# The G products of a feature-interaction tower as full-f32 half-height matmuls, with x's diagonal written by a mask product

## The reference

```python
for W in (W0, W1):
    Wr = W.reshape(m, Hk, Hn)                       # m = 39; Hk = 39, then 128; Hn = 128
    xk = jnp.einsum('bid,bjd,ijh->bhd', x0, xk, Wr)
    outs.append(xk)
z = jnp.sum(jnp.concatenate(outs, axis=1), axis=-1) # sum over d
h = relu(concat([z, dense_ctx]) @ W_top1 + b_top1)
h = relu(h @ W_top2 + b_top2)
y = h @ W_top3
```

## Time and profile before

| what | us |
|---|---|
| median of 3 runs (range) | 386.85 (385.5 to 388.55) |
| the profiled execution | 384.8 |
| its span | 383.0 |
| PE busy | 238.1 |
| DVE busy | 164.6 |
| ACT busy | 162.5 |
| POOL busy | 121.4 |

### The profile page before, as it was taken

How to read it: one execution, slowest core, us unless ns; L and a number is a source line. 1 busy time by engine, 2 the same in 40 slices (tenths; PEclk the granted TensorE clock), 3 DMA queues, 4 the chain that set the end, 5 groups by cost and what they waited for, 6 DMA issues and landing times. The chain is left out here.

```text
span 383.0 us, 4943 instructions
## 1 busy us (share of the span) xinstructions
PE 238.1 (62%) x1749; PEld 192.2 (50%) x1749; DVE 164.6 (43%) x336; ACT 162.5 (42%) x312; POOL 121.4 (32%) x119
## 2 busy tenths in 40 slices
PE   3662711011000011006988999999999999999997
PEld 2662400000000010004765778977799777888887
DVE  6943700000100000022887976755857656756211
ACT  6943510000000000014888577665868747756201
POOL 5987777777777777400000000000000000000000
PEclk9995765555555555555999999999999999999999
DMA  7600191000000000002020011000000100010000
GB/s 164 189 6 14 25 254 28 6 7 7 6 7 7 6 7 6 5 7 70 12 70 16 16 21 19 5 14 17 15 15 9 19 9 13 16 19 17 2 0 2
DMA packets 29094, 10.94 MB, mean 29 GB/s; under 512 B 21274, under 2 KB 27252, under 8 KB 29070
## 3 DMA queue, kind: packets, MB, share of 16 engines
q1 hardware_dynamic: 25390, 9.68, 11.0%
q0 software_dynamic: 3680, 0.95, 2.8%
HBM read 7.99 MB, written 0.00 MB: 21 GB/s over the span
## 5 line engine op out<-in xcount | busy, mean ns | idle before, releaser
L788 ACT ACTIVATE prod<-pair_bank 128x512 f32<-128x512 f32 (+1 forms) x112 | 66.1, 600 | 174.1 <-remote 119.8
L334 POOL DMA_INDIRECT emb<-tbl,ids_sb x115 | 121.2, 1054 | 37.2 <-issue 34.8
L414 PE MATMUL x_turn_bank<-tab_parts,later_hot 125*128 125x48 bf16 x160 | 12.5, 190 | 96.4 <-issue 95.7
L377 PE MATMUL x_bank<-prod_hi,pair_w_hi 128*128 128x512 f32 (+1 forms) x112 | 64.3, 574 | 6.9 <-issue 3.7
L651 DVE TENSOR_TENSOR prod_lo<-prod,prod_hi 128x512 fp32r<-128x512 f32 x96 | 65.0, 687 | 3.4
L414 PEld LDWEIGHTS x_turn_bank<-tab_parts,later_hot 125*128 125x128 bf16 x160 | 7.9, 100 | 102.1 <-issue 101.1
L359 PE MATMUL pair_bank<-x,sel 117*128 117x512 bf16 (+1 forms) x112 | 45.4, 406 | 9.7 <-issue 7.1
L641 DVE CAST prod_hi<-prod 128x512 fp32r<-128x512 f32 x48 | 20.4, 426 | 72.0 <-ACT prod L788 71.7
L633 DVE TENSOR_SCALAR later_hot<-later_ids,row_id 125x1024 bf16<-125x1024 f16 x20 | 9.7, 495 | 94.3 <-remote 94.2
L380 PE MATMUL x_bank<-prod_hi,pair_w_lo 128*128 128x512 f32 x96 | 38.9, 406 | 5.1 <-issue 5.1
L424 PE MATMUL turn_bank<-g_sb,w_sb 128*128 128x128 f32 x312 | 41.4, 275 | 0.6 <-ACT g_sb L820 0.6
(11 more groups left out here) (126 smaller groups left out, 307.1 us busy)
## 6 DMA issues: line engine op xcount, KB each, us to landing
xblk<-xs SPq DMA_DIRECT2D x128, 20.0 KB
emb<-tbl,ids_sb POOLq DMA_INDIRECT x115
tab<-small SPq DMA_DIRECT2D x2, 560.0 KB
wt<-w_top SPq DMA_DIRECT2D x2, 512.0 KB, 4.0
tab<-small SPq DMA_DIRECT2D x1, 504.0 KB
wa<-pair_w_a SPq DMA_DIRECT2D x1, 448.0 KB, 3.2
wb<-pair_w_b SPq DMA_DIRECT2D x1, 448.0 KB, 4.0
sel<-select SPq DMA_DIRECT2D x1, 204.8 KB
```

What stands on the lines that cost most here:

```text
L334: pool.indirect_dma_start(out=emb[:, at:at + D], out_offset=None, in_=tables[f], in_offset=bass.IndirectOffsetOnAxis(ap=ids_sb[:, c * M + ...
L377: mm = pe.matmul(x1_bank[:, :], pair_w_hi[p, t, :], hi(n), start=(t == 0), stop=(t == FULL))
L414: mm = pe.matmul(x1_turn_bank[:, f * 3 * D:(f + 1) * 3 * D], later_hot[:, r % HOT, f, :], tab_parts0[:, f, r, :, :], start=(r == 0 and f = ...
L788: act.activation(prod[0:ROWS[t], n % RING, :], pair_bank[n % 2][0:ROWS[t], :], ACT.Square).then_inc(sq_done, 1)
```

## The change

- **Layout of x3.** A group of 8 samples becomes two half groups of QB = 4. Turned rows of a group are now (half, d, b): rows 0 to 63 for four samples, rows 64 to 127 for the other four.
- **G.** `contract_d(k, pair)` takes two groups at a time. For each group and each half it issues one full-f32 matmul over 64 rows and 160 columns (4 samples x 40). The lower rows write `g_bank` 0, the upper ones `g_bank` 1. There is no hi/lo split. G_AT = (3, 6): both calls stand inside the same block's steps. A call waits for both copies (ACT's and DVE's) of the call before.
- **x's diagonal.** `spread_x` on DVE multiplies the turned x, repeated over four samples, with the mask `own` (128 x 4) and writes 128 x 4 x 4 x 39 numbers of `xblk` in one instruction. `xblk` is f32 with three buffers; its column of ones is written once from `own`. The 128 DMAs on SP, ACT's rounding of x, DVE's remainder of x and the zeroing of `xs` and `xblk` are gone.
- **x1.** ACT copies it to `x1_t` in f32; DVE's two remainder instructions are gone.
- **Copies of G.** ACT copies bank 0 and DVE bank 1 after each call, 128 x 320 each.

```diff
-G_AT = (3, 4, 6)
+G_AT = (3, 6)
...
+QB = GB // 2
+QC = MO * QB
+HALF = D * QB
+XBUFS = 3
...
-            def spread(k):
-
-                sp.wait_ge(xs_lo_done, k + 1)
-                wait(sp, g_mm, NG * (k - 1))
-                for b in range(GB):
-                    sp.dma_start(xblk[b::GB, k % 2, :, :, b, :].rearrange("p q g i -> p (q g) i").bitcast(F32),
-                                 xs[b::GB, k % 2, :, :, :].rearrange("p q g i -> p (q g) i").bitcast(F32)
-                                 ).then_inc(xblk_done[k % 2], 16)
...
-            def contract_d(k, g):
-                if g == 0:
-                    pe.wait_ge(x1_rounded, k + 1)
-                    pe.wait_ge(xblk_done[k % 2], SPREAD * (k // 2 + 1))
-
-                wait(pe, g_dve if g % 2 else g_act, 2 * k + g // 2)
...
+            def contract_d(k, pair):
+
+                if pair == 0:
+                    pe.wait_ge(x1_done, k + 1)
+                    pe.wait_ge(xblk_done, k + 1)
+
+                wait(pe, g_act, 2 * k + pair)
+                wait(pe, g_dve, 2 * k + pair)
+                for at in range(2):
+                    g = 2 * pair + at
+                    for half in range(2):
+                        rows = slice(half * HALF, (half + 1) * HALF)
+                        mm = pe.matmul(g_bank[half][:, at * QC:(at + 1) * QC], x1_t[rows, g * H:(g + 1) * H],
+                                       xblk[rows, k % XBUFS, g, :, :].rearrange("p b i -> p (b i)"), start=True, stop=True)
+                mm.then_inc(g_mm, 1)
...
+            def spread_x(k):
+
+                dve.wait_ge(xt_done, k + 1)
+                wait(dve, g_mm, 2 * (k - XBUFS + 1))
                 x_turned = misc_bank[:, 0:NG * MO].rearrange("p (g i) -> p g i", g=NG)[:, :, 0:M]
-                dve.tensor_tensor(xs[:, k % 2, 1, :, 0:M], x_turned, xs[:, k % 2, 0, :, 0:M],
-                                  ALU.subtract).then_inc(xs_lo_done, 1)
-
-            def take_x1_lo(k):
-                dve.wait_ge(x1_rounded, k + 1)
-                for half in (slice(0, NG // 2 * H), slice(NG // 2 * H, NG * H)):
-                    dve.tensor_tensor(x1_lo[:, half], x1_turn_bank[:, half], x1_hi[:, half],
-                                      ALU.subtract).then_inc(x1_done, 1)
...
+                dve.tensor_tensor(xblk[:, k % XBUFS, :, :, 0:M], x_turned.unsqueeze(2).to_broadcast([128, NG, QB, M]),
+                                  own[:, :].unsqueeze(1).unsqueeze(3).to_broadcast([128, NG, QB, M]),
+                                  ALU.mult).then_inc(xblk_done, 1)
```

More of the change, by code:

```diff
@@ L103, in build_tower @@
         parts = sb("parts", [128, D, 3, M], BF16)
-        x3 = sb("x3", [P3, 2, NB * NG, D, GB], BF16)
-        xs = sb("xs", [128, 2, 2, NG, MO], F32R)
-        xblk = sb("xblk", [128, 2, 2, NG, GB, MO], F32R)
+        x3 = sb("x3", [P3, 2, NB * NG * 2, D, QB], BF16)
+        own = sb("own", [128, QB])
+        xblk = sb("xblk", [128, XBUFS, NG, QB, MO])
         with ExitStack() as early:
@@ L268, in lo, with g_cols, g_bank_cols @@
             return prod_lo[:, n % RING2, :] if n % NT < FULL else prod_hi[32:64, n % RING2, :]
-        def g_cols(k, g):
-            b0 = (k % NB) * BB + g * GB
-            return g_sb[:, k // NB % 2, :, b0:b0 + GB]
+        def g_cols(k, pair, half):
+            b0 = (k % NB) * BB + pair * 2 * GB
+            return g_sb[:, k // NB % 2, :, b0:b0 + 2 * GB].rearrange("p i (g h b) -> p i g h b", g=2, b=QB)[:, :, :, half, :]
+        def g_bank_cols(half):
+            return g_bank[half][:, 0:2 * QC].rearrange("p (g b i) -> p i g b", g=2, b=QB)
         block = ctx.enter_context(nc.Block())
@@ L290, in _ @@
             sp.dma_start(row_id[:, :, :], row_ids).then_inc(row_id_in, 16)
+            sp.dma_start(own[:, :], own_row).then_inc(own_in, 16)
             for n, (f0, w, rows) in enumerate(SETS):
@@ L303, in _ @@
             sp.dma_start(idf[:, :], ident_f).then_inc(idf_in, 16)
[L304 to L308, removed]
+            for k in range(3):
+                sp.wait_ge(xblk_done, k + 1)
                 if k == 0:
@@ L362, in turn_x @@
             def turn_x(k):
-                wait(pe, xs_lo_done, k)
+                wait(pe, xblk_done, k)
                 pe.wait_ge(x3_b, k // NB + 1)
@@ L384, in turn_x1 @@
                 pe.wait_ge(x1_kept, k + 1)
-                wait(pe, x1_done, 2 * k)
+                wait(pe, x1_done, k)
                 c, j = divmod(k, NB)
@@ L479, in step @@
                     select_pair(n)
-                if u == 0 and k >= 2:
-                    contract_d(k - 2, 3)
                 if m >= 0:
@@ L567, in _ @@
             step(TILES + 3)
-            contract_d(K - 2, 3)
             mlp2(NCH - 2)
@@ L571, in _ @@
             mlp3(NCH - 2)
-            pe.wait_ge(xs_lo_done, K)
+            pe.wait_ge(xblk_done, K)
             for m in range(M1):
                 h1_part(NCH - 1, m, 0, True)
-            for g in range(NG):
-                contract_d(K - 1, g)
+            for pair in range(2):
+                contract_d(K - 1, pair)
             layer2(NCH - 1, 0, M)
@@ L930, in _ @@
             keep_x1h(K - 1)
-            keep_g(K - 2, 2)
+            keep_g(K - 2, 1)
             relu2(NCH - 2)
```

103 lines of the change are left out of this document (36 added, 67 removed).

## The result

The changed kernel takes 403.68 us (median of 4 runs, 400.32 to 407.23) against 386.24 us for the kernel before (4 runs, 385.5 to 388.55): a ratio of 1.040, 95% interval 1.035 to 1.046. It is slower, by far more than the 1% that was forecast. That the time lies inside the forecast's range, 374 to 404 us, is luck: the range reached so far for halves that run one after the other, and that is not what happened. The ratios in this text compare only runs within 1.5% of the fastest of their kernel, the medians take all runs. The profiled execution took 400.32 us with a span of 398.5 us, against 383.0 us before.

The account below looks back on a forecast made before the run. PE was taken to bound the dense part; the slow stretch had no named cause. Terms of +9.5, -1.0, -2.2 and -2.0 summed to +4.3 us on the median of 386.85, about 391 us, range 374 to 404 us.

Parts of the forecast that it names:

- The slow stretch: Early stretch of nearly idle PE: 16 fewer SP DMAs of x give back a few turns, -2 us, ends 0 and -6.
- The start: Chunk 0's gathers: without the memset of `xblk` that holds POOL, all comes earlier, -2.2 us, ends 0 and -2.3.
- A call's eight records: PE in `contract_d`: eight f32 records cost 0.79 us a call, ends 0.70 and 1.12, without changes of height.
- The change of height: PE around each `contract_d` call: going to 64 rows and back costs 0.19 us each, 0.39 us a call.
- +9.3 us stood for thirty: Thirty calls of `contract_d` in the dense part, each 1.18 us against 0.87 us before: +9.3 us.
- In the rest of chunk 0 ... -1.0 us together: From 174.3 to 209.0 us: three blocks gain 0.3 us each on ACT, PE's idle absorbs some new work; ends 0 and -3.
- The tail: The last block's two calls of G and their copies, with nothing overlapping: 3.16 us against 2.96, +0.2 us.
- Behind 209 us this is hidden: Dense part: savings of 0.36 us a block on DVE and 0.296 on ACT lie under PE and are worth nothing.
- Serial halves: Rival in `contract_d`: the two halves don't work side by side, 1.51 us a call, 401 us in all; chance 0.25.
- Cheap change of height: Rival in `contract_d`: 64 rows cost no change of height and the halves overlap, 0.70 us a call, 376 us; chance 0.18.
- The stretch hangs on SP's DMAs of x: Rival: the slow stretch goes with those DMAs, up to 120 us of its 127.5, leaving about 270 us; chance 0.08.
- for what I don't see: Remaining chance of 0.07, for example a slower copy of G or x3, or a longer slow stretch.

Follow-up runs that it names:

- f2: The kernel before, unchanged, run once more with its own trace on the next chip: 387.7 us.
- e2: The kernel before with the second memset of `xblk` moved ahead of the one-hots, into idle DVE time: 395.35 us, ratio 1.025.
- e1: The changed kernel with the 2.19 us memset put back on DVE behind the one-hots, into a tile nobody reads: 390.6 us.
- e7: The kernel before without the indirect gathers of chunks 1 to 3 (one plain DMA per chunk instead): 253.5 us.
- e3: The changed kernel without the indirect gathers of chunks 1 to 3 (one plain DMA per chunk instead): 265.4 us.
- f1: The changed kernel, unaltered, run once more on the next chip: 402.9 us, ratio 1.048.
- e14: The changed kernel without gathers of chunks 1 to 3, each product of G over all 128 rows: 1.09 us a call, no whole time given.
- e15: The changed kernel without gathers of chunks 1 to 3, all products of G over rows 0 to 63: 1.28 us a call, no whole time given.
- e13: The changed kernel with a POOL memset of 128 x 512 ahead of each gather of chunks 1 to 3, on another chip: 305.1 us, ratio 1.135.
- f3: The changed kernel with at most two gathers in flight and, from chunk 1 on, each tied to the tiles: 300.9 us, ratio 0.772.

## Why the prediction was wrong, point by point

- **The slow stretch ("PE's instructions before and inside it stay what they are", "-2 us, ends 0 and -6"): the step that failed.** The instructions stayed, the stretch's place among them did not. It began at 20.2 us, inside the third lookup, in place of 46.8, and put some 19 us of dense work behind it; with an end 4.6 us earlier that is +14.4 us where -2 stood. (In f2 the start moved by 20 us and block 0 did not, with the third lookup and nearly all touch matmuls through. So it is the work caught, and not the time of the start alone.) The profile of before had what was needed and I used it for another term only: the earlier trace rows show POOL held for 2.3 us just as the third lookup runs, and POOL's gathers as the only thing that goes on through the whole stretch (84.87 us busy in the earlier trace rows). I took the hold for a pure loss and asked only what an earlier gather gains, not what it collides with.
- **The start ("-2.2 us")**: that the memset holds a gather was right: without it the gather at 18.11 us takes 0.95 us. It is the 8th, not the 7th that the prediction named as its sign; the 7th takes 6.30 us there, as the 6th took 7.88 before. The last gather of chunk 0 is 4.3 us earlier, 2.3 us by the hold and the rest mostly because one gather more is issued ahead of 18 us. The worth was of the wrong sign: by block 0's transposes the hold saved 11.5 us in e2 (190.29 against 178.75) and 12.4 in e1 (193.17 against 180.73).
- **A call's eight records ("I take the middle of these two, 0.79 us")**: 0.55 us. Both estimates were too high. The lower one assumed that four records can't pair fully in this order, the other that two weight loads stand no closer than 0.11 us; that spacing is of loads into the same rows.
- **The change of height (2 x 0.19)**: 0.38 us measured, against 0.39. The row of a 16-row matmul priced a 64-row one within 0.01 us.
- **So a call costs 0.93 us and not 1.18**, where +9.3 us stood for thirty. The 0.87 us of before was too low as well. It took both groups at 0.43 us; the group behind `turn_x` costs 0.53, since its first matmul takes 0.24 us and not 0.15 (the chain of waits, before):

```profile
213.71 0.11 PE misc_bank L367 x4
213.82 0.24 PE g_bank L403
214.06 0.14 PE g_bank L404
214.21 0.15 PE g_bank L407
```

  So two groups cost 0.92 us on the mean. Blocks 8 to 15 give +0.5 us for 14 calls, about +0.04 a call or +1 us for thirty.
- **"In the rest of chunk 0 ... -1.0 us together"**: not shown. The blocks' +1.3 is made of -1.4 over blocks 0 to 3 (31.6 us before, 30.2 after), +1.6 at block 4 and +1.0 over blocks 4 to 15 (139.7 and 140.7 us). Of these the first doesn't repeat: it is -0.6 between e7 and e3, and +0.9 between f2 and f1. From block 0 to block 15 these pairs give +2.0 and +2.6 us.
- **The tail ("+0.2 us")**: from the start of the last block's G to the end of the last copy 2.84 us against 2.96, -0.1.
- **"Behind 209 us this is hidden"**: not in one place. In block 4 the one-hots of the next chunk stand behind the mask product and a copy of G in DVE's queue, and PE waits 1.68 us for one where it waited 0.73; the granted clock dips behind it (0.76 from 233 to 240 us). From block 3 to block 4 it is 12.0 us before and 13.6 after; in f2 and f1, without the dip, 12.0 and 12.9.

```profile
233.16 0.37 PE L409 MATMUL x_turn_bank<-tab_parts,later_hot 125*128 125x48 bf16 x8 [1.68 <-DVE later_hot L626]
```

- **The rivals.** "Serial halves" is refuted by e14 and e15. "Cheap change of height" is refuted as to its mechanism, but its price (0.70 us) was a little nearer to 0.93 than mine (1.18). "The stretch hangs on SP's DMAs of x" is refuted by the changed kernel itself, which has none of them and 149.5 us of the stretch; its time of 270 us is near what e3 and e7 gave when the gathers went, and what the kernel before took on one chip. What happened was in the 0.07 "for what I don't see", as "a longer slow stretch". The test I named ("wrong if the slow stretch differs by more than 6 us") is met: 149.5 against 127.5 us. So is the other, that the dense part be 6 to 10 us longer: it is 1.3 us longer by the blocks.

The page "TensorEngine Tiling (Array Packing)" of the Trainium skill states under "Key Properties" that a change of mode drains TensorE and that tiles can run their weight loads and matmuls in parallel. The runs agree with both halves, at 0.19 us a change and 0.55 against 1.09 us a call.

## What stays open

What the gathers and the instruction supplies share isn't named by any row. The trace's packets that carry instructions don't show it either: in the changed kernel one such packet starts between 22 and 175 us (8 KB at 50.3 us, 0.71 us long), so PE does not wait for one slow transfer of them after the other. Why that start of PE's work, the third lookup and the touch matmuls, matters more than what follows was not tested. On the chips where the kernel before takes 387 us the number in flight and the pitch were never moved apart (e13 ran on another). Why one chip of those used ran the kernel before in 269 us wasn't found; no trace of that kernel was taken there, and the changed kernel wasn't run there. Whether the version of f3 can be made better on both kinds of chip was not tried.

## What to carry to other kernels

When a profile shows one engine idle with "issue" as its reason, first ask which stream runs about as long as that idleness, and what work of the idle engine stands ahead of it, and treat their order as something that your change can move: an edit that only relieves that stream's engine can then cost more than all that it saves. A stream of small gathers may be worth slowing down: spreading the same 101 gathers over the tiles made the kernel 20% faster than before (0.795, 0.780 to 0.809) on a chip where the stretch exists, and a similar bound made it 6.6% slower on one where it doesn't, so both must be measured. Half-height f32 products on the two halves of the array are worth twice their rate, less 0.19 us each time the height changes.

## What the hardware showed that was not expected

- While POOL issues indirect gathers at a pitch of 1.25 us, PE's and SP's instructions come late: on PE 94 matmuls in 149.5 us (at first in groups of some five, 1.5 us apart, as at 20.88 and 22.34 us above), and in one run ACT's and DVE's too. Without the gathers of chunks 1 to 3 the long stretch is gone, and at a pitch of 2.6 us PE was not slowed. The slowness outlasts the last gather by 16 to 18 us (157.9 to 174.3 before, 152.1 to 169.7 after), though its data is there after 2.0 us.
- The low granted clock is not part of it: 145 us of it ran at 1.00 in f1.
- A 2.19 us memset on DVE, there for its zeros, was worth 12 us at block 0 by its side effect on POOL.
- The same kernel took 387 us on some chips and 269 us on another.
- Full-f32 products in the two halves of the rows overlap completely (0.55 against 1.09 us).
